# A Perceiver block pair on one core: Retention's last batch in parts, query projections inside unit 0, the last rows finished one stage later

## The reference, cut to what matters

```python
qkvg = layernorm(x) @ w_attn                 # 16 query heads, 8 key and value heads of 64, 8 gates
log_G = cumsum(log_sigmoid(6.906768 + gates))
s = rope(q) @ rope(k).T / 8
a = exp(2*log|s| + log_G[t] - log_G[s] - max)   # causal; so a = (|s| * decay)^2 / max^2
num = a @ v;  den = sum(a)
y = num / (den + 1e-6)
y = (y - mean(y)) / sqrt(var(y) + 1e-9) * ln_w   # per head, over 64
x = x + y.reshape(T, 1024) @ w_proj
```

## Time and profile before

| | us |
|---|---|
| median of 3 runs (2246.71 to 2252.75) | 2248.92 |
| the profiled execution | 2253.44 |
| its span | 2251.7 |
| TensorE busy (14773 instructions) | 2120.6 (94%) |
| VectorE busy | 1410.6 (63%) |
| ScalarE busy | 1376.8 (61%) |
| GpSimd busy | 296.0 (13%) |

### The profile page before, as it was taken

One profiled execution on the slowest core, in us unless ns is written; L12 is line 12 of the kernel. 1 busy time (PEld: TensorE's weight loads), 2 busy tenths in 40 slices (PEclk: granted clock), 3 DMA queues, 4 the chain that ended last, 5 costly groups with the idle time before them and its releaser, 6 DMA issues. The chain is left out here.

```text
span 2251.7 us, 37885 instructions
## 1 busy us (share of the span) xinstructions
PE 2120.6 (94%) x14773; PEld 1635.5 (73%) x14773; DVE 1410.6 (63%) x2399; ACT 1376.8 (61%) x2644; POOL 296.0 (13%) x268
## 2 busy tenths in 40 slices
PE   6999999999988987799999989999999999977998
PEld 4777787777864655688888856777877787756776
DVE  5555455555554775499999954555455454577887
ACT  3666566566652543388888835665665666554774
POOL 1111112122110000100000201121111121101001
PEclk9999999999997998899999989999999999988999
DMA  4001001010103012599999930100101010012996
GB/s 159 20 20 39 20 22 37 20 38 20 39 20 147 1 38 97 213 366 373 365 358 359 370 107 20 39 20 21 37 20 39 20 39 20 20 57 97 357 360 242
DMA packets 53776, 262.07 MB, mean 116 GB/s; under 512 B 9560, under 2 KB 9944, under 8 KB 26976
## 3 DMA queue, kind: packets, MB, share of 16 engines
q1 hardware_dynamic: 47296, 244.45, 29.0%
q0 software_dynamic: 2560, 8.39, 1.1%
q10 hardware_dynamic: 3744, 6.82, 0.8%
HBM read 243.65 MB, written 15.99 MB: 115 GB/s over the span
## 5 line engine op out<-in xcount | busy, mean ns | idle before, releaser
L613 DVE COPY c_pt<-bank 128x512 f32<-128x512 f32 x256 | 177.1, 692 | 557.5 <-PE bank L428 557.4
L813 ACT ACTIVATE c_pr<-wide,c_nmax 128x512 f32<-128x512 f32 x512 | 349.3, 697 | 147.5 <-DVE c_nmax L605 76.8
L295 POOL TENSOR_TENSOR c_clo<-land,c_chi 128x512 fp32r<-128x512 f32 x120 | 154.5, 1290 | 1007.0 <-ACT c_chi L782 911.9
L428 PE MATMUL bank<-ident,c_pr 128*128 128x128 f32 x2048 | 268.1, 274 | 2.7 <-ACT c_pt L820 1.4
L428 PEld LDWEIGHTS bank<-ident,c_pr 128*128 128x128 f32 x2048 | 239.8, 141 | 37.1 <-DVE c_pt L613 2.3
L796 ACT ACTIVATE c_khi<-bank,c_cols 128x512 fp32r<-128x512 f32 x128 | 88.1, 688 | 252.2 <-PE bank L95 252.2
L93 PE MATMUL bank<-c_wv_hi,c_chi 128*128 128x512 f32 x512 | 217.7, 425 | 18.4 <-DVE c_clo L544 17.1
L93 PE MATMUL bank<-c_chi,c_wk_hi 128*128 128x512 f32 x512 | 214.0, 418 | 0.3 <-DVE c_wk_lo L536 0.2
L94 PE MATMUL bank<-c_wv_lo,c_chi 128*128 128x512 f32 x512 | 202.6, 396 | 0.0
L95 PE MATMUL bank<-c_chi,c_wk_lo 128*128 128x512 f32 x512 | 202.4, 395 | 0.0
L95 PE MATMUL bank<-c_wv_hi,c_clo 128*128 128x512 f32 x512 | 202.3, 395 | 0.0
(11 more groups left out here) (416 smaller groups left out, 4270.1 us busy)
## 6 DMA issues: line engine op xcount, KB each, us to landing
moe_hr<-in_L_ffn_w SPq DMA_DIRECT2D x68, 1024.0 KB, 7.5
land<-in_L_ffn_w SPq DMA_DIRECT2D x34, 1024.0 KB, 7.8
land<-in_ctx SPq DMA_DIRECT2D x31, 1024.0 KB, 4.9
moe_raw<-in_L_ffn_w SPq DMA_DIRECT2D x18, 1024.0 KB, 7.8
moe_raw<-in_L_ffn_we_gate SPq DMA_DIRECT2D x8, 1024.0 KB, 6.8
land<-in_L_ffn_we_up SPq DMA_DIRECT2D x8, 1024.0 KB, 6.6
moe_raw<-in_L_ffn_we_down SPq DMA_DIRECT2D x8, 1024.0 KB, 6.7
moe_raw<-in_L_ffn_we_up SPq DMA_DIRECT2D x7, 1024.0 KB, 7.4
```

Source lines behind the costliest of these rows:

```text
L295: nc.gpsimd.tensor_tensor(clo[:, g % 2, c, :], raw[:, c, :], f32(chi[:, g % 2, c, :]), ALU.subtract) \
L428: last = pe.transpose(TB[n % 2][:, h * P:(h + 1) * P], pr[:, u % 2, h, n * P:(n + 1) * P], k["ident"][:])
L613: nc.vector.tensor_copy(pt[:, n, :], TB[0][:]).then_inc(pt_dve, 1)
L813: nc.scalar.activation(pr[:, u % 2, h, :], S[h][:], ACT.Exp, bias=nmax[:, b % 2, i, at:at + 1], scale=-1.0 if masked else 1.0, accum_out=d ...
```

## The change

In both cross-attentions query part 1 is projected inside unit 0, behind scores(0), which wait for part 0 alone; VectorE evacuates parts 1 to 3 after the maxima of unit 0; the banks of the parts are other ones. The first layer's last 128 rows are added and measured in the Retention stage, between the normalisation of batch 0 and those of the others. In Retention ln_w is a column that ScalarE multiplies into the output weights once, behind batch 0's copies (weigh_output); standardise works on the undivided numerators; the last batch is cut: squares by groups of four heads with the reciprocal as their scale, standardise and the output by halves, output(2) behind numerators(3), and the root and scaling of batch 2 later. TensorE waits for GpSimd's constants at sum_decay, not at the stage's start. In the last experts two VectorE steps change places.

```diff
-        QB = (S[2], S[3], OB, TB[1])
+        QB = (S[2], OB, TB[1], TB[0])
-                pool.wait_ge(q_done, 2)
+                pool.wait_ge(q_done, 1)
 def project_q(o):
-                    if o == 3:
+                    if o > 0:
                         pe.wait_ge(q_done, 1)
                         pe.wait_ge(v_done, 2)
 def scores(u):
-                        pe.wait_ge(q_done, max(u + 1, 2))
+                        pe.wait_ge(q_done, u + 1)
 def turn_p(u, n):
                     if u == 0 and n == 0:
-                        pe.wait_ge(v_done, 2)
-                    if u == 0 and n == 1:
                         pe.wait_ge(q_done, C)
 # TensorE
                 project_k(0, 1)
-                project_q(1)
...
                     if u == 0:
+                        project_q(1)
                         project_q(2)
 # VectorE
-                keep_q(1)
...
                     if u == 0:
-                        keep_q(2)
-                        keep_q(3)
+                        for c in range(1, C):
+                            keep_q(c)
...
-                    finish(NB - 1)
-                    dve.wait_ge(out_read, NB)
-                measure_rows(nc, s, k, x, NB - 1, norm)
                 if norm:
+                    measure_rows(nc, s, k, x, NB - 1, True)
 # Retention: SyncE
-                sp.dma_start(lnw[:], t["L0_attn_ln_w"].partition_broadcast(P)).then_inc(S["const_in"], 16)
+                for i in range(P // RD):
+                    sp.dma_start(lnw[i * RD:(i + 1) * RD, :], t["L0_attn_ln_w"].rearrange("(d o) -> d o", o=1),
+                                 allow_slow_non_contiguous=True).then_inc(S["lnw_in"], 16)
 # Retention: TensorE
 def sum_decay(b):
                     pe.wait_ge(S["cut"], b + 1)
+                    pe.wait_ge(S["filled"], 4)
 def numerators(b):
-                    pe.wait_ge(S["squared"], b + 1)
                     for i in range(4):
+                        pe.wait_ge(S["squared"], 4 * b + (i + 1 if b == NB - 1 else 4))
 def output(b):
+                    turn_y(0)
+                    if b < NB - 1:
+                        turn_y(1)
+                    multiply(0)
+                    if b == NB - 1:
+                        turn_y(1)
+                    multiply(1).then_inc(S["out_made"], 1)
-                pe.wait_ge(S["filled"], 4)
...
                     if b + 1 < NB:
                         project(b + 1)
-                    else:
-                        output(b - 1)
                     numerators(b)
-                    if 0 < b < NB - 1:
+                    if b > 0:
                         output(b - 1)
 # Retention: ScalarE
+                def last_squares():
+                    act.wait_ge(S["r_ready"], NB)
+                    for i in range(4):
+                        for h in range(4 * i, 4 * i + 4):
+                            last = nc.scalar.activation(s_abs[:, h, :], u[:, h, :], ACT.Square, scale=ru[:, h:h + 1])
+                        last.then_inc(S["squared"], 1)
+                        if i > 0:
+                            keep_a_part(NB - 1, i - 1)
+                    keep_a_part(NB - 1, 3)
+                def weigh_output():
+                    act.wait_ge(S["wp_in"], 16)
+                    act.wait_ge(S["lnw_in"], 16 * (P // RD))
+                    for c in range(2 * C):
+                        nc.scalar.activation(wp[:, c, :], wp[:, c, :], ACT.Identity, scale=lnw[:, 0:1]).then_inc(S["wp_done"], 1)
-                nc.scalar.sqrt(std[:], ve[:]).then_inc(S["std"], 1)
+                nc.scalar.sqrt(std[:, early], ve[:, early]).then_inc(S["std"], 1)
                 keep_xT(0)
+                act.wait_ge(S["final"], 1)
+                nc.scalar.sqrt(std[:, final], ve[:, final]).then_inc(S["std"], 1)
...
+                        squares(b)
                     else:
-                        keep_y(b - 1)
-                    squares(b)
+                        deviations(b - 1, 0, QH)
+                        last_squares()
                     if more:
                         keep_projection(b + 1, 3)
                         keep_projection(b + 1, 4)
-                    keep_a(b)
+                        keep_a(b)
+                    if b == 0:
+                        weigh_output()
                     if more:
                         gates(b + 1)
...
-                    deviations(b)
+                    if b + 2 < NB:
+                        deviations(b, 0, QH)
+                keep_y(NB - 2)
+                for i in range(2):
+                    deviations(NB - 1, i * KVH, KVH)
                 keep_y(NB - 1)
 # Retention: VectorE
+                    if b == NB - 1:
+                        nc.vector.reciprocal(ru[:], um[:]).then_inc(S["r_ready"], 1)
+                    else:
...
+                def standardise(b, at, n):
+                    for i, four, num in groups:
                         dve.wait_ge(S["num"], 4 * b + i + 1)
+                        s.mark(nc.vector.reduce_sum(col[:, 0, four], num[:, :, 0:RD], AX.X))
+                        s.mark(nc.vector.tensor_scalar_add(col[:, 1, four], num[:, :, RD], 1e-6))
+                    s.wait()
+                    s.mark(nc.vector.tensor_scalar(col[:, 2, heads], col[:, 0, heads], 1.0 / RD, None, ALU.mult))
+                    s.then(nc.vector.scalar_tensor_tensor(out=col[:, 3, heads], in0=col[:, 1, heads], scalar=1e-9, in1=col[:, 1, heads],
+                                                          op0=ALU.mult, op1=ALU.mult))
+                    for i, four, num in groups:
+                        nc.vector.tensor_tensor(yc[:, four, :], num[:, :, 0:RD],
+                                                col[:, 2, four].unsqueeze(2).to_broadcast([P, 4, RD]), ALU.subtract).then_inc(S["num_read"], 1)
...
                 dve.wait_ge(S["std"], 1)
-                s.then(nc.vector.reciprocal(rstd[:], std[:]))
+                s.then(nc.vector.reciprocal(rstd[:, 0:NB - 1], std[:, 0:NB - 1]))
+                normalise(0)
+                s.then(nc.vector.tensor_tensor(x[:, NB - 1, :], x[:, NB - 1, :], ps[7][:], ALU.add))
+                s.then(nc.vector.bn_stats(k["stats"][:, NB - 1, :], x[:, NB - 1, :]))
+                s.then(nc.vector.bn_aggr(mv[:, NB - 1, :], k["stats"][:, NB - 1, :]))
+                nc.vector.tensor_scalar_add(ve[:, NB - 1:NB], mv[:, NB - 1, 1:2], LN_EPS).then_inc(S["final"], 1)
+                for b in range(1, NB - 1):
+                    normalise(b)
...
+                    if b + 1 < NB:
+                        standardise(b, 0, QH)
+                        if b > 0:
+                            add_output(b - 1)
+                        if b + 2 < NB:
+                            scale(b, 0, QH)
+                scale(NB - 2, 0, QH)
+                for i in range(2):
+                    standardise(NB - 1, i * KVH, KVH)
+                    scale(NB - 1, i * KVH, KVH)
+                add_output(NB - 2)
 # last experts: VectorE
+                        if g + 1 < NG:
+                            low(0, g + 1)
                         if 1 <= g < NT - 1:
                             low_x(g + 1)
-                        if g + 1 < NG:
-                            low(0, g + 1)
```

More of the change, by code:

```diff
@@ L945, in stage_retention @@
                   "scores", "abs", "r_ready", "squared", "a_turned", "a_copied", "num", "num_read", "yvar", "ystd", "y_ready",
-                  "y_turned", "y_copied", "out_made", "res", "stored"):
+                  "y_turned", "y_copied", "lnw_in", "wp_done", "sums", "final", "out_made", "res", "stored"):
             S[n] = m.sem(n)
@@ L1067, in output, with turn_y @@
                 def output(b):
-                    pe.wait_ge(S["y_ready"], b + 1)
-                    flat = y2[:].rearrange("p h d -> p (h d)")
-                    for i in range(2):
+                    flat = y[:].rearrange("p h d -> p (h d)")
+                    def turn_y(i):
+                        pe.wait_ge(S["y_ready"], 2 * b + i + 1)
                         for j in range(4):
@@ L1073, in output, with multiply @@
                         last.then_inc(S["y_turned"], 1)
-                    pe.wait_ge(S["wp_in"], 16)
-                    pe.wait_ge(S["decay_exp"], 2 * min(NB, b + 2))
-                    for c in range(2 * C):
-                        if c % 4 == 0:
-                            pe.wait_ge(S["y_copied"], 2 * b + c // 4 + 1)
-                        last = pe.matmul(ps[6][:], yT[:, c, :], wp[:, c, :], start=(c == 0), stop=(c == 2 * C - 1))
-                    last.then_inc(S["out_made"], 1)
-                pe.wait_ge(S["filled"], 4)
+                    def multiply(i):
+                        pe.wait_ge(S["wp_done"], 2 * C)
+                        pe.wait_ge(S["y_copied"], 2 * b + i + 1)
+                        for c in range(4 * i, 4 * i + 4):
+                            last = pe.matmul(YB[b][:], yT[:, c, :], wp[:, c, :], start=(c == 0), stop=(c == 2 * C - 1))
```

(57 more changed lines are left out.)

44 lines of the change are left out of this document (14 added, 30 removed).

## The result

The changed kernel takes **2232.71 us** (median of 11 runs, 2227.52 to 2241.24), the kernel before 2246.71 (11 runs beside them, 2237.20 to 2252.75). The medians are 14.0 us apart. The ratio of the two sets is 0.9947 with a 95% interval of 0.9933 to 0.9962, which is 11.9 us less, between 8.5 and 15.1. The forecast was 11.0. The profiled execution took 2237.39 (span 2235.6); that of before 2253.44 (2251.7). Both lie 5 to 7 us above their medians, 16.1 us apart.

A forecast was written before the change was run, and what follows sets the result against it. TensorE, 94% busy, was taken as the bound. Terms 5.8+4.0+3.3+1.3-9.1+4.5+1.2 = 11.0 us (-9.1 is scaling, net), taken off the median 2248.92, gave 2238 us, range 2229 to 2246.

The forecast's parts named there:

- Unit 0: Both cross-attentions: scores no longer wait behind the second query's projection; 5.8 us gained in the first, 4.0 in the second.
- Seam: Entry into Retention: first normalisation starts earlier, 3.3 us gained; less half clock in the first projection, 1.3 more.
- Scaling: Retention batch 1: eight output-weight scalings delay scores and bring low clock, 10.7 us lost; decay-sum waits return 1.6.
- Rival 1: Batch 1: the clock stays up through the longer gap, 5.7 us more gained, 2232 us; chance 0.20.
- rival 2: Batch 1's gap: clock falls and stays low through batch 2's projection and batch 0's output, 2257 us; chance 0.06.
- Last batch: Retention's last batch: squares by head, output by halves and batch 2's output behind the numerators gain 4.5 us.
- last copy 836.6, numerators done 839.6: Last batch: predicted trace times in us for the last copy after the squares and the end of the numerators.
- Rival 4: Last batch by halves gains nothing, as small instructions and half-width column steps eat the overlap; 2242.4 us; chance 0.12.
- Experts: Last layer's experts: weights' low part first ends the pair sooner, three TensorE waits shrink; 1.2 us gained.

The follow-up runs named there:

- before_again: The kernel before, unchanged, profiled a second time; this execution's span is 2239.5 us.
- e2_spread: Changed kernel with the eight scalings of output weights moved, four and four, into ScalarE's idle gaps ahead of batch 1's projection copies; 2222.62 us, ratio 0.9902 to before.
- e5_seam_swap: Kernel before plus only the last rows finished in Retention, the constants awaited at the decay sums, and the experts' two low parts exchanged; ratio 0.9953 to before.
- e3_ahead: Changed kernel with batch 2's output again ahead of the last numerators, its root and scaling made earlier; ratio 0.9920 to before.
- e9_whole_late: e2_spread with one whole product and one whole square in the last batch, batch 2's output still behind the numerators; ratio 0.9901 to before.
- e7_copy: e3_ahead and e2_spread together, plus the first half's copy of turned y ahead of the second half's root on ScalarE; ratio 0.9898 to before.
- e8_whole: e7_copy with one whole VectorE product and one ScalarE square in place of the last batch's 16 small squares; ratio 0.9884 to before.
- e4_busy: Changed kernel with products nobody reads put on TensorE in two gaps, of batch 1 and of the last batch; ratio 0.9944 to before.
- e11_gaps: e8_whole with the last batch's product and square in two halves, plus unread products filling two Retention gaps; 2211.91 us, ratio 0.9849 to before.

## Why the prediction was right, and where it was not

The total was right: 11.0 forecast, 11.9 measured by the ratio (8.5 to 15.1) and 14.0 by the medians. The signs of the terms were right too as far as they could be read, but one term was nearly all wrong, and how the trace terms add up to the total depends on which profile of before is taken. Part of the hit is luck.

- **Unit 0, 5.8 and 4.0.** Right in mechanism and size against the profile it was read from. The first term contains a stretch of low clock that the second profile of before has for less long: 2.7 there. The second is 4.0 in both (from the end of key 1 to unit 1: 21.0 us before and in before_again, 17.0 after and in e2_spread).
- **Seam, 3.3 and 1.3.** The wait measured 3.6. The half clock of the first projection went whole, 2.8, in four of ten traces and by some 1.2 in six, so 1.3 was a fair middle. In return the clock falls ahead of batch 0's decay sums (3.78 us in e5_seam_swap, 2.95 in before_again). In sum 3.0 to 5.4 against before_again.
- **Scaling, -10.7 and +1.6.** The step was right throughout: 5.01 us for the eight, scores of batch 1 5.5 later against batch 0's numerators, then 6.51 and 9.69. The trace shows -10.3, and e2_spread gives 10 us back by moving eight instructions. Rival 1, a clock that stays up, is out: the scores take 6.51 in the changed kernel and in e3_ahead, which keeps the scalings there. So is rival 2: the clock rises again within the projection. For the waits of the decay sums 1.6 were forecast, and that stretch gained 2.0.
- **Last batch, 4.5.** Gained 0.3. The step that failed is "last copy 836.6, numerators done 839.6". Moved back by the lead of 10.8, the last copy is forecast at 825.8 and ends at 826.2: right. But the numerators are forecast to be done at 828.8 and end at 832.3 (825.36+6.93), since transposes and numerators were counted at full clock and ran at half: 2.28 instead of 1.12 and 6.93 instead of 3.68. That is 3.5 of the 4.2 us that are missing. y's transposes and batch 2's product, 2.0 and 7.1 to 9.1 in the forecast, took 1.91 and 8.32, and the two halves of output 3 took 9.8 (851.98-842.23) instead of 8.9. The forecast's own times leave TensorE idle for some 6 us ahead of the transposes (from about 824.3 to 830.4), and I didn't ask what that does to the clock, as I had in batch 1. Rival 4 gave that outcome (0) for another reason, small instructions. Their durations were near the forecast (16 squares and four copies in 7.7 us, forecast 7.4), and the harm was in pacing TensorE. The stretches of the four combinations show that neither the order nor the small squares alone make the 42 us: 40.8 with small squares and the output behind (e2_spread), 38.5 with whole squares and the output behind (e9_whole_late), 38.4 with small squares and the output ahead (e7_copy), 33.9 with whole squares and the output ahead (e8_whole). e7_copy and e8_whole also have the early copy of the half, which the other two lack.
- **Experts, 1.2.** Open. The last line of the table adds 0.8, but the waits that the term was built on didn't shrink (7.4 before, 7.6 after).

So the terms don't add up to the total in one way. Against the first profile of before, the last batch was forecast 4.2 too high, while the seam and batch 0 gave 7.3 more than forecast (1.9 and 5.4 in the table) and the other lines 2.0 more: 16.1. Against before_again the changed kernel's trace is only 3.9 ahead. What lies between is mostly low clock that comes in some executions of before and not in others, in unit 0 and in batch 0. The measured 11.9 lies between the two, and that it came out so near to 11.0 owes something to this.

The new standardising reads PSUM twelve times a batch. VectorE's sums of 128x256 out of PSUM took 0.42 us, as much as a 128x256 product out of SBUF, and its additions of 128x4 out of PSUM took 0.15, where steps of 128x16 in SBUF took 0.17. The prediction cites a rule for such reads (the Trainium skill, "VectorE: DVE Perf Modes", TRN2 errata), 65 ns more for a PSUM source than for an SBUF source. These rows don't show it, and it would have changed the sum by 0.3.

## What to carry to other kernels

Whoever adds a wait of TensorE has to ask what runs at half clock behind it, and also where instructions of another engine let TensorE go a few at a time. Here 16 small squares, in place of one large product with one large square, let the numerators start 1.1 us sooner in one order and 1.9 later in the other, and cost 2.3 and 4.5 us in all. Work that is needed only much later (here a scaling of weights, 5 us) belongs into gaps of its engine that the trace shows; that was worth 10 us for moving eight instructions. And one profile is one execution: before a term is built on a stretch of low clock, see a second profile.

## What the runs showed that I had not expected

- A product of 128x512 in this type, issued once, is two instructions of 0.44 us each (28 of them in 12.28 us for 14 products). What each of the two does, no run shows.
- The clock fell again behind 4.6 us of thin transposes that stood 2.4 us in two waits, after 12 us without a pause (e4_busy). It stayed at 1.00 through a gap of 3.5 us that was filled (e11_gaps, 692 to 704).
- Two executions of the kernel before, with waits alike to 0.02 us, differ by 3.1 us in unit 0 and 6.8 from the first cross-attention's last products to batch 0's numerators, through the clock alone. With the new seam the same stretch has 49.8 to 57.3 in ten traces.
